# Slot attention before a mixture of experts: units of two batches in place of halves of four, and where the maxima stand

## The reference, cut to what matters

```python
Pn = rmsnorm(P, input_norm_w)
k_proj = Pn @ Wk.T
v_proj = Pn @ Wv.T
for _ in range(3):
    sn = rmsnorm(slots, slot_norm_w)
    q_proj = sn @ Wq.T
    scores = jnp.einsum('bkd,bmd->bkm', q_proj, k_proj) * SCALE
    attn = jax.nn.softmax(scores, axis=-2)
    attn = attn / (jnp.sum(attn, axis=-1, keepdims=True) + EPS)
    updates = jnp.einsum('bkm,bmd->bkd', attn, v_proj)
    slots = gru_cell(updates, slots, gru_wih, gru_whh, gru_bih, gru_bhh)
```

## Time and profile before

| | us |
|---|---|
| median of three runs | 690.17 |
| lowest, highest | 689.04, 697.9 |
| the profiled execution | 688.93 |
| its span, first to last instruction | 686.8 |

### The profile page before, as it was taken

The page is one execution under the profiler, slowest core; times in us unless marked ns, Lnnn a source line. Parts: engine busy times, 40 slices in busy tenths (PEclk is TensorE's granted clock), DMA queues, the critical chain, the costliest instruction groups (busy, mean ns, idle before and its releaser), DMA issues.

```text
span 686.8 us, 15058 instructions
## 1 busy us (share of the span) xinstructions
PE 517.0 (75%) x5128; PEld 393.9 (57%) x5128; DVE 386.8 (56%) x1032; ACT 321.0 (47%) x917; POOL 211.1 (31%) x385
## 2 busy tenths in 40 slices
PE   3968977877779967977898788789877550599940
PEld 2622345555535436877787677768776440599940
DVE  0599755665365435777777676777778351022212
ACT  2546834443212227676777566767677210232210
POOL 8293722123100002333333324332443006100025
PEclk9988979998979978999999899999999965699975
DMA  9976544341699550000006996000000791200012
GB/s 297 231 192 158 145 160 112 112 113 44 138 246 211 123 244 1 3 1 3 1 0 141 229 224 128 2 2 1 0 0 2 311 422 43 77 16 16 16 32 69
DMA packets 46837, 73.29 MB, mean 107 GB/s; under 512 B 4614, under 2 KB 40375, under 8 KB 45639
## 3 DMA queue, kind: packets, MB, share of 16 engines
q1 hardware_dynamic: 42588, 59.93, 34.1%
q0 software_dynamic: 1472, 8.72, 3.5%
q10 hardware_dynamic: 2730, 4.03, 1.9%
HBM read 69.06 MB, written 3.60 MB: 106 GB/s over the span
## 4 chain that ended last, share of the span: by engine, by line
PE 51%; DVE 15%; POOL 10%; issue 9%; DMA 6%; ACT 6%; POOLq 1%; SPq 1%; ACTq 0%; DVEq 0%
PE ps L1528 9%; PE ps L1543 7%; PE ps L1667 4%; PE ps L1465 4%; PE ps L1657 4%; DMA work<-in_kv_blk 4%; PE ps L1373 3%; POOL work L672 2%; PE ps L1499 2%; POOL xe_scratch L704 2%; PE ps L1564 2%; POOL early_w L709 2%; PE ps L1553 2%; PE ps L1345 2%; PE ps L1402 2%
## 5 line engine op out<-in xcount | busy, mean ns | idle before, releaser
L817 ACT ACTIVATE work<-ps,nb,rkey 125x56 f32<-125x56 f32 x576 | 174.7, 409 | 49.7 <-PE ps L1543 37.1
L1528 PE MATMUL ps<-work,region 128*64 128x96 f32 (+1 forms) x2304 | 114.6, 253 | 7.3 <-DVE work L1211 7.3
L1528 PEld LDWEIGHTS ps<-work,region 128*64 128x64 f32 (+1 forms) x2304 | 102.9, 139 | 17.5 <-ACT work L817 9.1
L1543 PE MATMUL ps<-region,work 125*64 125x129 f32 x1152 | 74.1, 278 | 26.0 <-POOL work L672 26.0
L1543 PEld LDWEIGHTS ps<-region,work 125*64 125x64 f32 x1152 | 64.9, 138 | 29.0 <-POOL work L672 29.0
L672 POOL TENSOR_TENSOR work<-work,rs 125x336 f32<-125x336 f32 x96 | 71.8, 748 | 7.5
L1150 DVE TENSOR_REDUCE mx<-ps 125x6 f32<-125x336 f32 x96 | 47.9, 499 | 23.9 <-PE ps L1528 23.0
L670 POOL TENSOR_TENSOR rs<-rs,rkey 125x6 f32<-125x6 f32 x96 | 19.2, 201 | 133.5 <-DVE rs L1165 133.5
L1161 DVE TENSOR_REDUCE sm<-work 125x6 f32<-125x336 f32 x96 | 47.5, 495 | 3.9 <-ACT work L817 3.7
L1153 DVE SCALAR_TENSOR_TENSOR nb<-mx,rkey 125x6 f32<-125x6 f32 x96 | 43.8, 457 | 3.3
L709 POOL DMA_INDIRECT early_w<-ys_scratch,gidx x14 | 13.4, 956 | 82.1 <-DMA ys_scratch<-folded 78.1
(11 more groups left out here) (297 smaller groups left out, 925.8 us busy)
## 6 DMA issues: line engine op xcount, KB each, us to landing
region<-in_w SPq DMA_DIRECT2D x6, 2048.0 KB, 18.2
region<-in_ctxT SPq DMA_DIRECT2D x16, 750.0 KB
early_w<-in_ctx SPq DMA_DIRECT2D x16, 672.0 KB
region<-in_ctx SPq DMA_DIRECT2D x16, 672.0 KB
work<-in_ctxT_blk SPq DMA_DIRECT2D x22, 187.5 KB
early_w<-in_w POOLq DMA_DIRECT2D x1, 4096.0 KB, 12.4
region<-in_ctx_blk ACTq DMA_DIRECT2D x11, 187.5 KB
early_w<-in_ctx_blk ACTq DMA_DIRECT2D x10, 187.5 KB
```

The costliest lines, as they stand in the source:

```text
L817: i = act.activation(shares_of(a, h)[:, c, :], ps[:CP, 2 + 2 * a + h, c * S:(c + 1) * S], ACT.Exp, bias=nb[:, a, q:q + 1], scale=rkey[:, b ...
L1528: mm = pe.matmul(ps[r0:r1, 2 + 2 * a + h, c * S:c * S + WIDE], keysT[:, k * QB + s, c0 + r0:c0 + r1], qT[:, k, s * S:s * S + WIDE], start= ...
L1543: mm = pe.matmul(ps[i * COL:(i + 1) * COL, 6 + p, 0:KW], A[:CP, i, h, c * S:c * S + COL], keys[:, k * QB + 2 * p + i, h * CH + c, :], star ...
```

## The change

The half of 4 batches becomes a *unit* of 2 batches, 4 steps. Four pairs take turns: unit c of a group works on pair c modulo 4, 12 units a group, 24 in all. Units 0, 1, 10 and 11 of a group are written out; 2 to 9 are a loop of two turns with four units in it. Accumulators alternate between banks 6 and 7.

The cell and the queries work on 112 columns, once per unit, in place of 224 once per phase. They are spread over the two units after their own: in unit v+1 PE starts the cell after the update of step 1, with the gates in step 2; ACT takes the gates in step 2 and the candidate in step 3, each behind that step's exponentials; DVE scales the accumulator in step 0, takes the inputs in step 2 and the candidate at the end of step 3. In unit v+2 DVE writes the new slots in step 0, PE projects in step 1, POOL and DVE take the norm in steps 2 and 3, PE transposes the queries at the end of step 3; DVE scales them in step 0 of unit v+3, and the scores of unit v+4 read them. The projection and the queries now stand in the accumulator bank of the unit before (columns 0 to 255 and 256 to 367), so the projection waits for the scaling of that accumulator and for the queries before the last.

The maxima of a step no longer go to `mx` in SBUF but to columns 400 to 405 of the step's own score bank, where the second operation reads them.

```diff
-QB = GB // 2
-QS = QB * S
+TWO = GB // 2
+QS = 2 * S
 ITERS = 3
-HB = 2 * QB
+STEPS = 4
 CH = CC // 2
 LOOK = 3
-PHASES = 2 * ITERS
+UNITS = TWO * ITERS
+LAST = GROUPS * UNITS - 1
 KW = 129
 WIDE = 96
 COL = 64
...
         def phases(eng, phase):
             for g in range(GROUPS):
-                phase(g, 0, g * PHASES)
-                with eng.Fori(0, ITERS - 1) as it:
-                    for w in (1, 2):
-                        phase(g, w, eng.snap(it * 2 + (g * PHASES + w)))
-                phase(g, PHASES - 1, g * PHASES + PHASES - 1)
-        def step_of(m):
-            p, h, i = m // 4, m // 2 % 2, m % 2
+                for c in (0, 1):
+                    phase(g, c, g * UNITS + c)
+                with eng.Fori(0, 2) as it:
+                    for c in range(2, 6):
+                        phase(g, c, eng.snap(it * TWO + (g * UNITS + c)))
+                for c in (UNITS - 2, UNITS - 1):
+                    phase(g, c, g * UNITS + c)
...
+        def steps_ahead(g, c, m):
+            over = (c + m // STEPS) // UNITS
+            return (g + over, (c + m // STEPS) % TWO, m // STEPS, m % STEPS) if g + over < GROUPS else None
+        def step_of(p, m):
+            h, i = divmod(m, 2)
             return 2 * p + i, h, i
-        def quad(g, k):
-            return slice((g * 2 + k) * QS, (g * 2 + k + 1) * QS)
+        def cell_runs(g, c):
+            return g > 0 or c > 0
+        def cell_ends(g, c):
+            return g > 0 or c > 1
+        def leaves(c):
+            return c < 2 or c >= UNITS - 2
+        def renews(g, c):
+            return c < UNITS - 2 or g + 1 < GROUPS
+        def pair(g, p):
+            return slice((g * TWO + p) * QS, (g * TWO + p + 1) * QS)
...
-                        sp.wait_ge(u_mm, (g * PHASES - 2) * HB + s // 2 * 4 + 4)
+                        sp.wait_ge(u_mm, (g * UNITS - TWO + s // 2 + 1) * STEPS)
...
+            def phase(g, c, v_):
+                for m in range(STEPS):
+                    to = steps_ahead(g, c, m + 1)
+                    if to:
+                        weigh(to[0], to[1], v_ + to[2], to[3])
+                    if m == 2 and renews(g, c):
+                        slot_rms(v_ + 2, c % 2)
+                    if m == 3:
+                        if c == UNITS - 2 and g + 1 < GROUPS:
                             key_rms(g + 1, 0)
-                        if w == 0 and g:
-                            key_rms(g, 1)
+                            key_rms(g + 1, 1)
+                        if c == UNITS - 1 and g + 1 < GROUPS:
+                            key_rms(g + 1, 2)
+                        if c == 0 and g:
+                            key_rms(g, 3)
...
-            def phase(g, w, u):
-                k = w % 2
-                for m in range(HB):
-                    if m == 0 and (g, w) != (0, 0):
-                        gates_of(u - 1)
-                    if m + LOOK < HB:
-                        exponentials(g, k, u, m + LOOK)
-                    elif prepares(g, w):
-                        exponentials(g + w // (PHASES - 1), 1 - k, u + 1, m + LOOK - HB)
-                    if m == 0 and (g, w) != (0, 0):
-                        candidate_of(u - 1)
-                    if m == 1 and prepares(g, w):
-                        slot_sums(u + 1)
+            def phase(g, c, v_):
+                for m in range(STEPS):
+                    to = steps_ahead(g, c, m + LOOK)
+                    if to:
+                        exponentials(to[0], to[1], v_ + to[2], to[3])
+                    if m == 1 and renews(g, c):
+                        slot_sums(v_ + 2, c % 2)
+                    if m == 2 and cell_runs(g, c):
+                        gates_of(v_ - 1)
+                    if m == 3 and cell_runs(g, c):
+                        candidate_of(v_ - 1)
...
+                mx = ps[:CP, 2 + 2 * a + h, 400:400 + CH]
                 v.wait_ge(a_mm, n + 1)
-                v.tensor_reduce(mx[:, a, c], ps[:CP, 2 + 2 * a + h, 0:CH * S].rearrange("p (c s) -> p c s", s=S),
+                v.tensor_reduce(mx, ps[:CP, 2 + 2 * a + h, 0:CH * S].rearrange("p (c s) -> p c s", s=S),
                                 AX.X, ALU.max).then_inc(a_max, 1)
                 v.wait_ge(a_max, n + 1)
-                v.scalar_tensor_tensor(nb[:, a, c], mx[:, a, c], -1.0, rkey[:, b, c], ALU.mult, ALU.mult).then_inc(a_neg, 1)
...
-            def phase(g, w, u):
-                k = w % 2
-                gru = (g, w) != (0, 0)
-                for m in range(HB):
-                    if m == 0 and gru:
-                        update(u - 1, 1)
-                        gru_inputs(u - 1)
-                    if m + 1 < HB:
-                        attention(g, k, u, m + 1)
-                    elif prepares(g, w):
-                        attention(g + w // (PHASES - 1), 1 - k, u + 1, 0)
-                    if m + LOOK < HB:
-                        maxima(g, k, u, m + LOOK)
-                    elif prepares(g, w):
-                        maxima(g + w // (PHASES - 1), 1 - k, u + 1, m + LOOK - HB)
-                    if m == 4 and prepares(g, w):
-                        queries(u + 1, 1 - k)
-                    if m == 0 and gru:
-                        gru_candidate(u - 1)
-                    if m == 1:
-                        if w in (0, PHASES - 1):
-                            if gru:
-                                finish(u - 1, g - (w == 0), 1 - k)
-                            if loads_next(g, w):
-                                v.tensor_copy(slots_x[:, 1 - k, :], xln[:, quad(g + (w > 0), 1 - k)]).then_inc(sl_ok, 1)
-                        else:
-                            gru_slots_new(u - 1, 1 - k, slots_x[:, 1 - k, :]).then_inc(sl_ok, 1)
-                    if m == 4:
-                        update(u, 0)
-                    if m == 2 and prepares(g, w):
-                        slot_norm(u + 1)
+            def phase(g, c, v_):
+                old = (c - 2) % TWO
+                for m in range(STEPS):
+                    if m == 3 and renews(g, c):
+                        slot_norm(v_ + 2, c % 2)
+                    to = steps_ahead(g, c, m + 1)
+                    if to:
+                        attention(to[0], to[1], v_ + to[2], to[3])
+                    if m == 0 and (g, c) != (0, 0) and (c == 0 or renews(g, c - 1)):
+                        queries(v_ + 1, (c + 1) % TWO, 6 + c % 2)
+                    if m == 2 and cell_runs(g, c):
+                        gru_inputs(v_ - 1)
+                    to = steps_ahead(g, c, m + LOOK)
+                    if to:
+                        maxima(to[0], to[1], v_ + to[2], to[3])
+                    if m == 0:
+                        if cell_ends(g, c):
+                            if leaves(c):
+                                finish(v_ - 2, g - (c < 2), old)
+                            else:
+                                gru_slots_new(v_ - 2, old, slots_x[:, old, :]).then_inc(sl_ok, 1)
+                        if leaves(c) and renews(g, c):
+                            first_slots(g + (c >= 2), old)
+                        if cell_runs(g, c):
+                            update(v_ - 1, 6 + (c + 1) % 2)
+                    if m == 3 and cell_runs(g, c):
+                        gru_candidate(v_ - 1)
...
+            def gru_start(v_, p):
                 if not isinstance(v_, int) or v_ > 0:
                     pe.wait_ge(gru_v, v_ * 2)
+                pe.wait_ge(un_ok, v_ + 1)
+                pe.matmul(ps[:, 1, 0:QS], UnN, pair_rows, start=True, stop=True)
                 for gate in range(2):
                     pe.matmul(ps[:, 0, gate * QS:(gate + 1) * QS], whh[:, gate * D:(gate + 1) * D],
-                              slots_x[:, k, :], start=(gate == 0), stop=False, skip_group_check=True)
-                pe.matmul(ps[:, 1, QS:2 * QS], whh[:, 2 * D:3 * D], slots_x[:, k, :], start=True, stop=True)
-                pe.wait_ge(un_ok, (v_ + 1) * 2)
-                for p in range(2):
-                    mm = pe.matmul(ps[:, 1, 2 * p * S:2 * (p + 1) * S], UnN[:, p, :], pair_rows, start=True, stop=True)
-                mm.then_inc(ut_mm, 1)
+                              slots_x[:, p, :], start=(gate == 0), stop=False, skip_group_check=True)
+                pe.matmul(ps[:, 1, QS:2 * QS], whh[:, 2 * D:3 * D], slots_x[:, p, :], start=True, stop=True).then_inc(ut_mm, 1)
...
+            def slot_proj(x, p, bank):
+                pe.wait_ge(sl_ok, x + 1)
+                if not isinstance(x, int) or x >= 3:
+                    pe.wait_ge(un_ok, x - 2)
+                if not isinstance(x, int) or x >= 2:
+                    pe.wait_ge(q_ok, x - 1)
+                pe.matmul(ps[:QS, bank, 0:256], slots_x[:, p, :],
+                          GI[:, :, :].rearrange("p a d -> p (a d)"), start=True, stop=True).then_inc(q_proj, 1)
...
-            def phase(g, w, u):
-                k = w % 2
-                gru = (g, w) != (0, 0)
-                for m in range(HB):
```

(64 more changed lines are left out.)

207 lines of the change are left out of this document (86 added, 121 removed).

## The result

The changed kernel took 668.27 us in the median of four runs, 0.963 of the kernel before (95% interval 0.956 to 0.971; 693.53 on that occasion). Forecast: 666, faster.

A forecast was written before the change was run, and what follows sets the result against it. An in-order PE meeting the cell's chain bounds the kernel; phases -22, transition -1, last phase -1, tail -1.3, first +2 give about -23.5 from 688.93, 665.4, stated as 666 for the median; range 655 to 683.

The forecast's parts named there:

- The two waits that it wanted to remove: PE's waits for POOL's weighing and for the new slots: together 20.9 us in 200, 2.4 per phase.
- the cell's chain: Update, cell, projection, norm and queries, which have only five steps to run in; in-order PE meets them.
- PE's work: PE's own instructions in a unit: 9.8 us, 19.6 per former phase, 1.1 more than before.
- The unit: One unit of the slot attention takes 10.25 us: 20.5 against 22.73 per phase, 2.2 saved.
- The ring that I named: PE's update, exponentials, candidate, new slots, accumulator scaling, projection: 10.2 us, so the projection waits 0.4 per unit for DVE.
- a second short wait ... in parallel: DVE's queries come late for the next unit's first scores, about 0.3 us, in parallel with the projection's wait.
- Rival B: POOL's multiplication holds DVE's candidate and slot operations, each up to 0.75 us: unit 11.0, whole 682; chance 0.20.
- it is on neither ring, so nothing of it counts by itself: Maxima in PSUM free 29 us of DVE's time in L1153, but by themselves save nothing.
- Ten former phases: Ten full phases at -2.2 us each are -22, and the transition between the groups -1.
- Copy to first scores: First unit: two projections, norms and queries in series ahead of the first scores, about +1 us.
- Tail: End of the slot attention: the last cell is half as wide, -1.3 us.
- Just in time: Second group's last key batch lands 56 us after the first byte and is wanted at 56.7.

The follow-up runs named there:

- the later candidate: The changed kernel with the cell's two candidate operations moved in DVE's order from the end of step 3 to step 0 of the next unit: 661.99 us, 0.952.
- e8: The changed kernel with the candidate operations moved to step 0 of the next unit, but the maxima in SBUF again: 677.76 us, 0.976.
- e7: The changed kernel with the candidate operations moved to step 0 of the next unit, and hn in PSUM as well: 661.96 us, 0.952.

## Why the prediction was right, point by point

The two waits that it wanted to remove are gone, and that is not luck. The closeness of the number, 1 us in 24, is: it took misses of opposite sign and a second ring of nearly the same length.

**What bounded.** An in-order PE that met the cell's chain too early: confirmed. The two waits of the earlier trace rows are gone after the change.

**PE's work.** 9.8 us per unit from records priced by width; measured 9.79, the 10.03 of the later candidate less its wait of 0.24. The terms are off in both directions. The sixteen records of 112 columns took 2.22 us, 0.14 each, where 0.16 gave 2.54, and those of L1567, inside the cell's run, 0.11, the lower bound. The two updates took 2.86 in place of 2.66, the scores of four steps 4.22 in place of 4.08.

**The unit.** Forecast 10.25, measured 10.36 plain and 10.5 in the mean. The ring that I named, over the new slots into the projection, has some slack: the projection never waited in a plain unit, and its forecast wait of 0.4 was not there. The ring that binds is the one I passed over as "a second short wait ... in parallel", DVE's scaling of the queries. At the projection the slack is 0.2 us (0.30 from the scaling of the accumulator, where a waiting projection starts after 0.10), so the two are that near each other, and the number came out. With the candidate moved the forecast wait appears, at 0.24 us. Part of the ring behind it, over ACT's candidate, the slots and the accumulator, was right; its start was not, since the exponentials wait for the second maxima operation and not for the update. One reading in its sum was off by 0.07 us: the candidate overlaps its forerunner by 0.15 in the earlier trace rows (311.98 + 1.84 against 313.67), not by 0.08.

**Rival B in part.** The cover of the held L1153 did go, and the candidate is held for 0.29 us per unit, the first slot operation for 0.19. I had priced both at up to 0.75. By the timeline only the first lies on the ring, and its 0.29 is what the kernel with hn and nt in PSUM gave back; that kernel freed both, so it does not tell them apart. The Trainium skill, "SBUF — State Buffer", section "SBUF: two separate sides", has the pair of ports locked against a VectorE operation with two SBUF inputs; the traces agree: 96 of 96 operations with one of their two inputs in PSUM took 164 to 167 ns, the same operation with both in SBUF up to 718 (in e8).

**The step that failed.** "... it is on neither ring, so nothing of it counts by itself". In the new order it counts 15.2 of the 24.5 us by the stretches, 11 by the medians. I had followed the rings with L1153 at 0.17 everywhere and never with it held, so I could not see that three of them stand on the way round. The sum hid the error, since it assumed both parts at work; for the order alone it would have forecast 666 too, and 679 was measured.

**Terms of the sum.** Ten former phases, the group change included: 230.9 to 210.5 us by the projections, -20.4; forecast -23. First and last unit with the ramps: -3.5, forecast 0. Copy to first scores: 6.62 to 5.43, forecast +1. The second pair's queries do stand ahead of the first scores in PE's order (260.09, waiting for the second norm), but they come only 1.46 us behind the first pair's, since POOL takes the second pair's power while PE has the first pair's transposes, and each piece is half as wide. Another 0.5 of it is the clock: in the second trace of this kernel it stayed at 0.50 as before, and the same piece took 5.93. Tail: 7.78 to 8.41, forecast -1.3. DVE now has the output of the cell before ahead of the last accumulator, and 0.7 is the clock, granted at 0.68 in place of 0.97; at 1.00 (e7) the tail took 7.68. The misses cancel to 1 us, by luck.

**Keys.** Just in time was right: the last bytes moved by 416 us, the first scores of that batch came at 417.62, and no wait for them is in the trace. Their transfers cost in another way, by the stop. The clock between the groups, which the prediction left open, was 1.00 in the long unit, against 0.87 before.

## What to carry to other kernels

When VectorE and GpSimd release each other in a fixed order, as here, a port conflict need not be a matter of chance: it fell on the same instruction in every turn. Price a conflict by following the whole ring with it and without it, not by the idle time ahead of the held instruction. And test the parts of a change apart: here one gives nothing in the old order and most of the gain in the new one. Putting a small intermediate of two VectorE operations into a free corner of a PSUM bank cost nothing that shows in the time, and the second one was held no more. And an engine without a named wait is not yet the one that binds: a start that follows another engine's end by the same 0.10 us in every turn is a wait, though the profile calls it "issue".

## What had not been expected

VectorE's reduction into PSUM took 510 ns against 499 into SBUF, so such a write costs about 0.01 us. PE stopped inside a run of matmuls for 1.6 us, up to 2.8 in other traces, whose long units took 11.2 to 14.5 us, only while the keys were being loaded, and in the units written out between the loops or right behind them. And stages with the same code ended between 251.8 and 257.4 us in the profiled executions, a spread as large as the differences between the last variants.
